# Small gaps between tensors: weights, normed rows and gated product at other byte offsets

## The reference

```python
qkv  = silu(layernorm(x) @ qkv_w.T)             # 512 -> 3 * 4096
gate = sigmoid(layernorm(x) @ gate_w.T)         # 512 -> 4096
attn = decayed causal attention of q, k, v      # 32 heads of 128, 64 tokens
x = x + (gate * (norm_w * rms_norm(attn))) @ out_w.T
x = x + cross_attention(layernorm(x), ctx)
x = x + layernorm(x) @ identity.T
```

## Time and profile before

| | before |
|---|---|
| median of 3 runs (lowest, highest) | 2171.26 us (2170.05, 2172.16) |
| profiled execution, its time | 2172.25 us |
| its span, first to last instruction | 2170.4 us |
| mean granted TensorE clock | 0.992 of full speed |
| instructions | 42216, of them 16208 matmuls and 16208 weight loads |

### The profile page before, as it was taken

One profiled execution on the slowest core, in us unless ns is written; L12 is line 12 of the kernel. 1 busy time (PEld: TensorE's weight loads), 2 busy tenths in 40 slices (PEclk: granted clock), 3 DMA queues, 4 the chain that ended last, 5 costly groups with the idle time before them and its releaser, 6 DMA issues. The chain is left out here.

```text
span 2170.4 us, 42216 instructions
## 1 busy us (share of the span) xinstructions
PE 2106.2 (97%) x16208; PEld 1698.9 (78%) x16208; DVE 1421.6 (65%) x1989; ACT 1126.7 (52%) x1927; POOL 859.1 (40%) x882
## 2 busy tenths in 40 slices
PE   5999999999999999999999999999999999799998
PEld 5787888888888878787878787878888887466665
DVE  6666666565666666766666666666665655588885
ACT  4545555454545455554555555454554544366664
POOL 6534435352534443644353534444352632111110
PEclk9999999999999999999999999999999999799999
DMA  2311111111111111111111111011111111301110
GB/s 81 109 31 60 41 59 40 59 40 50 50 50 50 48 41 49 52 33 48 51 51 50 50 35 62 32 59 40 59 40 59 40 51 34 126 30 45 56 39 20
DMA packets 40502, 109.49 MB, mean 50 GB/s; under 512 B 4960, under 2 KB 9568, under 8 KB 40288
## 3 DMA queue, kind: packets, MB, share of 16 engines
q1 hardware_dynamic: 40128, 107.25, 15.2%
q10 hardware_dynamic: 288, 1.05, 0.1%
HBM read 104.09 MB, written 4.19 MB: 50 GB/s over the span
## 5 line engine op out<-in xcount | busy, mean ns | idle before, releaser
L836 PE MATMUL bank<-x_hi,w_lo 128*128 128x512 f32 x1344 | 529.4, 394 | 0.0
L836 PEld LDWEIGHTS bank<-x_hi,w_lo 128*128 128x128 f32 x1344 | 252.2, 188 | 61.7
L362 POOL TENSOR_TENSOR sq_acc<-sq_acc,sq 128x512 f32<-128x512 f32 x124 | 160.5, 1294 | 352.3 <-ACT sq L519 342.7
L831 PE MATMUL bank<-x_hi,w_hi_c 128*128 128x512 f32 x672 | 270.6, 403 | 2.5 <-DVE v L632 1.5
L834 PE MATMUL bank<-x_lo,w_hi_c 128*128 128x512 f32 x672 | 265.9, 396 | 0.0
L854 PE MATMUL bank<-w_lo,x_hi 128*128 128x256 f32 x896 | 252.7, 282 | 0.0
L888 PE MATMUL bank<-wo_hi,y_hi 128*128 128x512 f32 x512 | 204.7, 400 | 6.0 <-DVE y_lo L670 4.9
L351 POOL TENSOR_TENSOR qk<-qk,sq 128x512 f32<-128x512 f32 x64 | 83.0, 1296 | 307.9 <-ACT sq L486 307.9
L890 PE MATMUL bank<-wo_hi,y_lo 128*128 128x512 f32 x512 | 201.9, 394 | 0.0
L889 PE MATMUL bank<-wo_lo,y_hi 128*128 128x512 f32 x512 | 201.6, 394 | 0.0
L632 DVE TENSOR_TENSOR qk<-bank,qk 128x512 f32<-128x512 f32 x192 | 127.8, 689 | 85.2 <-ACT qk L488 42.6
(11 more groups left out here) (150 smaller groups left out, 4951.9 us busy)
## 6 DMA issues: line engine op xcount, KB each, us to landing
raw<-w_pairs SPq DMA_DIRECT2D x126, 512.0 KB, 3.6
raw_o<-w_out SPq DMA_DIRECT2D x32, 512.0 KB, 3.6
raw<-ctx_in SPq DMA_DIRECT2D x16, 256.0 KB, 3.0
raw<-ctx_in SPq DMA_DIRECT2D x32, 128.0 KB, 3.1
xr<-x SPq DMA_DIRECT2D x4, 1024.0 KB, 11.4
out<-attn_acc SPq DMA_DIRECT2D x16, 256.0 KB, 2.1
attn_acc<-x SPq DMA_DIRECT2D x8, 256.0 KB, 6.3
decays<-decay SPq DMA_DIRECT2D x32, 64.0 KB, 1.9
```

What stands on the lines that cost most here:

```text
L362: nc.gpsimd.tensor_tensor(acc, acc, sq[:, b, h], ALU.add).then_inc(sq_added, 1)
L831: nc.tensor.matmul(bank[:, to], w_hi[w][:, a, s], x_hi[:, b, c], start=part in ("first", "only") and c == 0, stop=False, skip_group_check= ...
L836: i = nc.tensor.matmul(bank[:, to], lo[:, a, s], x_hi[:, b, c], start=False, stop=part in ("last", "only") and c == 1, skip_group_check=True)
```

## The change

Tensors without a use are allocated between the others ("gaps"; sizes in the lists are in float32 elements, that is 352, 128, 416, 288, 480 and 64, 192, 448, 320 bytes, with 128 before x_hi and 384 before y_hi). No instruction is added, removed or reordered; the operands start elsewhere.

```diff
+GAPS = (88, 32, 104, 72, 120)
+HI_GAPS = (16, 48, 112, 80)
...
+        def placed(allocate, name, shape, k, **kind):
+            allocate(f"gap_{name}", [P, GAPS[k]])
+            return allocate(name, shape, **kind)
+
+        self.w_lo = [placed(same, f"w_lo{k}", [P, 7, 2 * P], k, dt=F32R) for k in range(4)]
+        self.wo_lo = placed(same, "wo_lo", [P, HG, D], 4, dt=F32R)
         close()
-        self.raw = [sb(f"raw{k}", [P, 7, 2 * P]) for k in range(4)]
-        self.raw_o = sb("raw_o", [P, HG, D])
+        self.raw = [placed(sb, f"raw{k}", [P, 7, 2 * P], k) for k in range(4)]
+        self.raw_o = placed(sb, "raw_o", [P, HG, D], 4)
...
+        sb(own, "gap_x", [P, 32])
         x_hi = sb(own, "x_hi", [P, 7, 2, BT], F32R)
         x_lo = sb(own, "x_lo", [P, 7, 2, BT], F32R)
-        w_hi = [sb(own, f"w_hi_{n}", [P, 7, 2 * P], F32R) for n in "abc"]
+        w_hi = []
+        for n, gap in zip("abc", HI_GAPS):
+            sb(own, f"gap_w_hi_{n}", [P, gap])
+            w_hi.append(sb(own, f"w_hi_{n}", [P, 7, 2 * P], F32R))
...
+        sb(own, "gap_wo_hi", [P, HI_GAPS[3]])
         wo_hi = sb(own, "wo_hi", [P, HG, D], F32R)
...
+        sb(own, "gap_y", [P, 96])
         y_hi = sb(own, "y_hi", [P, HG, BT], F32R)
```

More of the change, by code:

```diff
@@ L53, in __init__ @@
         self.consts = consts
-        self.w_lo = [same(f"w_lo{k}", [P, 7, 2 * P], F32R) for k in range(4)]
-        self.wo_lo = same("wo_lo", [P, HG, D], F32R)
+        def placed(allocate, name, shape, k, **kind):
[3 more added lines that the diff above has]
+        self.wo_lo = placed(same, "wo_lo", [P, HG, D], 4, dt=F32R)
         close()
-        self.raw = [sb(f"raw{k}", [P, 7, 2 * P]) for k in range(4)]
-        self.raw_o = sb("raw_o", [P, HG, D])
+        self.raw = [placed(sb, f"raw{k}", [P, 7, 2 * P], k) for k in range(4)]
+        self.raw_o = placed(sb, "raw_o", [P, HG, D], 4)
         self.ctx, self.crossed = (r[:, 0:4].rearrange("p (t r) n -> p t (r n)", t=2) for r in self.raw[:2])
```

## The result

Measured again side by side with the kernel before, the changed kernel takes 2167.12 us (median of 19 runs, 2164.2 to 2169.03) against 2170.92 us (19 runs, 2166.79 to 2172.3): the ratio is 0.9982 with a 95% interval of [0.9975, 0.999]. So it is 3.8 us faster, just short of the 0.2% that the prediction took as the bound between faster and the same. Forecast were 2170 us in a range of 2142 to 2185.

The account below looks back on a forecast made before the run. TensorE, busy 97% of the span, was taken to bound the kernel by its matmul pace. All terms summed to 0; the median, less 1 us for a slightly likelier faster rival, gave 2170 us, range 2142 to 2185.

Parts of the forecast that it names:

- Where time is spent: TensorE, busy 97% of the span: matmul steps sum to 1613 us, three quarters of it; waits are small.
- The term of TensorE's reads: Weight load beside streamed matmul: placement changes no rate, zero taken; bounds -137 us to +27 us.
- the prediction's own test: Projections: the prediction is wrong if one's mean step differs from 233.4 ns by more than 1.1 ns.
- rivals 1 and 3: TensorE's operand distances: 1, projections leave a bad pair, 2138 to 2167 us, chance 0.30; 3, worse pairs, 2175.5 to 2195, 0.26.
- The excess grows with the columns: TensorE's steps: 11.0 ns excess for 256 columns, 19.9 for 512, one load each, so no load clash.
- distance 0 holds in the slowest and in the fastest: Against a distance effect: distance 0 in two thirds of the slowest matmuls (233.4 ns) and all of the fastest (229.0).
- ACT, DVE, POOL, DMA taken as zero: Other engines and weight loads: no change; 15 us if DVE lost its cover, 13 us for DMA given no weight.
- The gain that G01's wait gives back: G01's wait for ACT, 0.60 us in 16 units: the 24 matmuls before it return their gain, 1.0 us at 2.5 ns each.
- Upper bound: TensorE's reads: at most 4.4 ns more per projection matmul, +17.7 us; with values and output +27 us.

Follow-up runs that it names:

- e6: Kernel before, own placement, but G01 loads only 64 and G23 only 32 of 128 weight columns per matmul; read for steps alone: 230.4 and 231.9 ns.
- e7: The same narrow loads (G01 64, G23 32 columns) on the placement of e3; read for steps alone: 230.0 and 232.2 ns.
- e3: Changed kernel with other gaps: all projections and the output at distances 256 (high part) and 0 (low part); 2149.11 us, ratio 0.9901 to the kernel before.

## Why the prediction held in its time and not in its reason

- *Where time is spent.* Right in the main: TensorE's pace between waits carried about 3 us of the 4, and 1.0 us was one pause in the first unit.
- *The term of TensorE's reads, taken as zero.* Wrong, and by the prediction's own test: it called itself wrong if a projection's step left 233.4 ns by more than 1.1, and three of six did (-4.0, -5.6, +1.6). What was said of rivals 1 and 3 was true in different projections at once, and partly cancelled. The time fell into the range because the six pairs of the change average 232.0 ns, 1.3 under the old pair: 5.4 us on 4032 matmuls, before the output and the wait took their part. That the sum came out near zero is luck: nothing in the prediction said that better and worse pairs would be mixed like this.
- *The argument that misled.* "The excess grows with the columns, so it isn't the load": e6 and e7 show that the stream's pace isn't its own matter: it changes with the width of the load beside it, or with what goes with that width. Two lengths of stream also differed in what was loaded and streamed, so they were no test of one cause. And "distance 0 holds in the slowest and in the fastest" looked at the high part alone: the slowest has its low part at 416, the fastest has both at 0, and both at 0 turned out as the good pair. The rows had pointed at it.
- *The pages.* By "SBUF — State Buffer" (Who interferes with whom) of the Trainium skill TensorE's read ports for the stream and for the weight load are independent, and it never waits on anyone. This case disagrees on the first: e3 against before is 21.0 us by the distance of its own two reads. The 213.5 ns of half the cold step, or the 215.7 ns that "TensorE: Matmul & The Clock Gate" gives, were reached by no placement; 226.7 was the lowest pace seen.
- *ACT, DVE, POOL, DMA taken as zero.* Right: busy times moved by 0.5 us at most and no new wait came.
- *The gain that G01's wait gives back.* Right in kind and near in size: it was to return what the 24 matmuls before it gain, 24 x 5.6 = 0.13 us a unit here, and the idle time grew by 0.08 in the unit shown and 1.4 us in all 16.
- *Upper bound.* The slowest pair found (235.5) is 2.2 ns over before, half of the 4.4 assumed.

Open: why a whole load at distance 0 modulo 256 makes the stream faster than a narrower one does, what the last 13.2 ns above 213.5 are, and how the start selects one of two paces.

## What to carry to other kernels

When TensorE is busy all the time, divide the distance of two matmul starts by their number and compare with half of the cold step; a surplus of some per cent in float32r streams can be placement. For 512-column streams put what is loaded and what is streamed at distance 0 modulo 256 bytes (here 226.7 instead of 233.3 ns). For the 256-column streams here that was the worst place (120.0 against 117.8 ns), so don't carry it over, and don't take one pair's rate for all of them: give each call its own pair once, read the rates of every unit from one profile, as a call can have two paces, then use the best. Where a tensor is loaded in one call and streamed in another, the two can want different distances, as here, and a few spare bytes with two views serve both.

## What the runs showed of the hardware that was not expected

- The pace of float32r matmuls (512 columns) depends on the distance of loaded and streamed operand with a period of 256 bytes: 226.7 to 235.5 ns. Moving all starts together by 96 bytes changes nothing (233.3 in either).
- The two placements compared differ only with the whole load of 128 columns: with 64 columns the step is 230.0 to 230.4, with 32 it is 231.9 to 232.2, at either.
- At one and the same placement a stream can keep either of two paces to its end: 113.3 or 117.8 ns at (64, 64) for 256 columns, 231.1 or 235.5 ns at (64, 32) for 512. In the second half of the tokens a single matmul of 96 columns ahead of it switched the pace; one of 32 in the first half didn't.
